# Queries and keys kept in DRAM by feature, with the heads' rows side by side

## The reference

```
xn = adaln(x, cond, ln1);  q, k, v = split(xn @ qkv_w.T);  q, k = rope(q), rope(k)
x  = x + attn(q, k, v) @ sa_out_w.T
xn = adaln(x, cond, ln2);  q = rope(xn @ q_w.T);  k = rope(context @ k_w.T);  v = context @ v_w.T
x  = x + attn(q, k, v) @ ca_out_w.T
xn = adaln(x, cond, ln3);  x = x + (gelu(xn @ ffn_w1.T + b1) @ ffn_w2.T + b2)
attn: softmax(q k' / sqrt(32)) v for each head;  adaln: LayerNorm, then x (1 + gamma) + beta with gamma, beta from cond
```

## Time and profile before

| what | value |
|---|---|
| median of three runs | 1928.59 us |
| profiled execution, its own time | 1925.28 us |
| its span, first to last instruction | 1923.5 us |
| mean granted clock of TensorE | 0.994 |
| PE busy | 1869.4 us (97%) |
| ACT, DVE, POOL busy | 72%, 67%, 41% |
| DMA packets | 306451, 308.37 MB |

### The profile page before, as it was taken

The page is one execution under the profiler, slowest core; times in us unless marked ns, Lnnn a source line. Parts: engine busy times, 40 slices in busy tenths (PEclk is TensorE's granted clock), DMA queues, the critical chain, the costliest instruction groups (busy, mean ns, idle before and its releaser), DMA issues. The chain is left out here.

```text
span 1923.5 us, 39339 instructions
## 1 busy us (share of the span) xinstructions
PE 1869.4 (97%) x13460; PEld 1630.4 (85%) x13460; DVE 1294.9 (67%) x2250; ACT 1383.3 (72%) x3813; POOL 785.8 (41%) x818
## 2 busy tenths in 40 slices
PE   8899999999998999999999998899999999999999
PEld 7788888888877888888888886688898998989898
DVE  7766676767776677676776776446667666666754
ACT  4777777888876888888888888655666666565654
POOL 3534433443442454454454441013536354444531
PEclk9999999999998999999999999999999999999999
DMA  7666676566576778767668677343232322323130
GB/s 232 195 203 185 204 223 194 177 200 198 165 220 189 204 212 233 201 197 227 199 200 225 198 217 190 109 137 110 78 99 67 99 88 89 95 71 110 45 99 33
DMA packets 306451, 308.37 MB, mean 160 GB/s; under 512 B 21072, under 2 KB 260048, under 8 KB 306256
## 3 DMA queue, kind: packets, MB, share of 16 engines
q1 hardware_dynamic: 304528, 304.47, 53.4%
q10 hardware_dynamic: 1728, 1.39, 0.3%
HBM read 212.46 MB, written 92.27 MB: 158 GB/s over the span
## 5 line engine op out<-in xcount | busy, mean ns | idle before, releaser
L744 ACT ACTIVATE ps_s<-ps_s,neg_max 128x256 f32<-128x256 f32 x1024 | 452.8, 443 | 55.4 <-DVE neg_max L861 48.3
L861 DVE TENSOR_REDUCE neg_max<-ps_s 128x2 f32<-128x512 f32 x512 | 349.3, 687 | 212.8 <-PE ps_s L615 212.4
L758 ACT ACTIVATE prob<-ps_s 128x512 f32<-128x512 f32 x512 | 303.4, 593 | 137.2 <-PE ps_s L634 134.3
L634 PE MATMUL ps_s<-qT,kT 98*128 98x256 f32 x1024 | 211.6, 289 | 24.4 <-DMA qT<-max_rows 21.8
L931 POOL TENSOR_TENSOR rope_c<-rope_c,rope_s 128x256 f32<-128x256 f32 x128 | 98.4, 769 | 330.5 <-DVE rope_s L836 330.5
L615 PE MATMUL ps_s<-kT,qT 96*128 96x256 f32 x1024 | 216.5, 293 | 10.7 <-ACT ps_s L744 8.3
L615 PEld LDWEIGHTS ps_s<-kT,qT 96*128 96x128 f32 x1024 | 169.9, 190 | 60.3 <-ACT ps_s L744 28.4
L605 PE MATMUL ps_g<-xx_hi,w_hi 128*128 128x256 f32 x1024 | 208.1, 285 | 1.4 <-issue 1.4
L634 PEld LDWEIGHTS ps_s<-qT,kT 98*128 98x128 f32 x1024 | 169.3, 191 | 46.9 <-issue 21.0
L744 ACT ACTIVATION_READ_ACCUMULATOR ps_s<-ps_s,neg_max 128x1 f32 x1024 | 207.8, 203 | 0.0
L605 PE MATMUL ps_g<-xx_lo,w_hi 128*128 128x256 f32 x1024 | 205.5, 282 | 0.0
(11 more groups left out here) (155 smaller groups left out, 4654.7 us busy)
## 6 DMA issues: line engine op xcount, KB each, us to landing
kT<-k_turned SPq DMA_DIRECT2D x384, 128.0 KB, 3.1
qT<-q_turned SPq DMA_DIRECT2D x128, 256.0 KB, 3.9
f_raw<-in_w1T SPq DMA_DIRECT2D x124, 256.0 KB, 3.1
k_turned<-rot_hi SPq DMA_DIRECT2D x64, 256.0 KB, 3.2
k_turned<-rot_lo SPq DMA_DIRECT2D x64, 256.0 KB, 2.5
q_turned<-rot_hi SPq DMA_DIRECT2D x64, 256.0 KB, 3.6
q_turned<-rot_lo SPq DMA_DIRECT2D x64, 256.0 KB, 4.1
qT<-q_turned SPq DMA_DIRECT2D x128, 128.0 KB, 3.9
```

The source lines that it names most:

```text
L634: ins = eng.matmul(ps_s[:, score_bank(step), t * L:(t + 1) * L], kT[:, quad % NQ, j, t * P:(t + 1) * P], qT[:, quad % NQ, j, :], start=Tru ...
L744: ins = eng.activation(scores[:, t * L:(t + 1) * L], scores[:, t * L:(t + 1) * L], ACT.Exp, bias=neg_max[G % 2][:, t, j:j + 1], accum_out= ...
L758: eng.activation(prob[:, n % NP, :, :].rearrange("p t l -> p (t l)"), ps_s[:, score_bank(step), :], ACT.Exp).then_inc(exp_done, 1)
L861: eng.tensor_reduce(neg_max[G % 2][:, :, j], ps_s[:, score_bank(step), :].rearrange("p (t l) -> p t l", l=L), AX.X, ALU.max, negate=True). ...
```

## The change

The DRAM tensors are laid out as (item parity, part, feature, head, position), so that the rows of one feature of neighbouring heads lie side by side. A spill is then two transfers for the high part and two for the low part, one for each half of the features: source 128 partitions of 1 KB, destination 8 heads x 16 features x 1 KB, with the heads outermost. A stack of queries is one transfer of 64 rows and one of 32 rows, in pieces of 4 KB. A stack of keys is one transfer whose source is the high part, repeated twice by an outermost dimension of size 2 and step 0, into 64 partitions, and one of 32 rows for the low part. The counts of the semaphores follow: 64 for an item's spills and not 32, two transfers for a stack of keys and not three.

```diff
-        turned = {m: nc.dram_tensor(f"{m}_turned", (2, D, 2, L), F32, kind="Internal").ap() for m in "qk"}
+        turned = {m: nc.dram_tensor(f"{m}_turned", (2, 2, HD, H, L), F32, kind="Internal").ap() for m in "qk"}
...
-            STACKS = {"q": 2, "k": 3}
+            STACKS = {"q": 2, "k": 2}
...
-                return spilled[m][t], 32 * (i + 1)
+                return spilled[m][t], 64 * (i + 1)
...
-                        out_to = turned[m][i % 2, T * t * P:T * (t + 1) * P].rearrange("(p d) s l -> s p d l", d=2)
+                        heads = slice(t * HG, (t + 1) * HG)
                         eng.wait_ge(rot_hi_done, n)
-                        eng.dma_start(out_to[0], rot_hi[:, n % NT, :, :].bitcast(F32)).then_inc(spilled[m][t], 16)
+                        for half in range(2):
+                            into = turned[m][i % 2, 0, half * HALF:(half + 1) * HALF, heads, :].rearrange("d h l -> h d l")
+                            eng.dma_start(into, rot_hi[:, n % NT, half, :].bitcast(F32)).then_inc(spilled[m][t], 16)
                         eng.wait_ge(rot_lo_done, n)
-                        eng.dma_start(out_to[1], rot_lo[:, n % NT, :, :].bitcast(F32)).then_inc(spilled[m][t], 16)
+                        for half in range(2):
+                            into = turned[m][i % 2, 1, half * HALF:(half + 1) * HALF, heads, :].rearrange("d h l -> h d l")
+                            eng.dma_start(into, rot_lo[:, n % NT, half, :].bitcast(F32)).then_inc(spilled[m][t], 16)
...
-                        eng.wait_ge(spilled[m][n // 2], 32 * (i + 1))
+                        eng.wait_ge(spilled[m][n // 2], 64 * (i + 1))
...
-                        heads = turned[m][i % 2][n * OH * HD:(n + 1) * OH * HD]
+                        high, low = (turned[m][i % 2, part, :, n * OH:(n + 1) * OH, :].rearrange("d j l -> d (j l)") for part in range(2))
+                        into = (qT if m == "q" else kT)[:, quad % NQ, :, :].rearrange("p h l -> p (h l)").bitcast(F32)
                         if m == "q":
-                            eng.dma_start(qT[0:2 * HD, quad % NQ, :, :].bitcast(F32),
-                                          heads.rearrange("(h d) s l -> (d s) h l", d=HD)).then_inc(stack_in[m][n], 16)
-                            eng.dma_start(qT[2 * HD:ROWS, quad % NQ, :, :].bitcast(F32),
-                                          heads[:, 0].rearrange("(h d) l -> d h l", d=HD)).then_inc(stack_in[m][n], 16)
+                            both = turned[m][i % 2, :, :, n * OH:(n + 1) * OH, :].rearrange("s d j l -> (s d) (j l)")
+                            eng.dma_start(into[0:2 * HD, :], both).then_inc(stack_in[m][n], 16)
+                            eng.dma_start(into[2 * HD:ROWS, :], high).then_inc(stack_in[m][n], 16)
                         else:
-                            for s in range(2):
-                                eng.dma_start(kT[s:2 * HD:2, quad % NQ, :, :].bitcast(F32),
-                                              heads[:, 0].rearrange("(h d) l -> d h l", d=HD)).then_inc(stack_in[m][n], 16)
-                            eng.dma_start(kT[2 * HD:ROWS, quad % NQ, :, :].bitcast(F32),
-                                          heads[:, 1].rearrange("(h d) l -> d h l", d=HD)).then_inc(stack_in[m][n], 16)
+                            eng.dma_start(into[0:2 * HD, :], high.unsqueeze(0).broadcast_to([2, HD, OH * L])).then_inc(stack_in[m][n], 16)
+                            eng.dma_start(into[2 * HD:ROWS, :], low).then_inc(stack_in[m][n], 16)
```

## The result

| kernel | median | ratio to before, 95% interval | span | granted clock |
|---|---|---|---|---|
| before | 1927.6 us | 1 | 1923.5 us | 0.994 |
| the change | 2336.4 us | 1.2116 [1.2091, 1.2140] | 2335.4 us | 0.921 |

The account below looks back on a forecast made before the run. PE bounds the kernel before; after the change, DMA engines 0 and 1 were to bound attention. Start 36, attention 1553 and feed-forward 688.5 give 2277.5 us; with 1.8 and 3.3 us added, 2283 us, range 2150 to 2440.

Parts of the forecast that it names:

- On how many engines a transfer runs: DMA transfers: the smaller outermost count rules; high keys on two engines, spills on eight, queries and low keys on 16.
- Narrow transfers share their engines: Narrow DMA transfers always land on the same first engines, giving engines 0 and 1 34.6 MB in attention.
- Two full engines set the pace: Attention: engines 0 and 1, 96% full at 23.2 GB/s, stretch it to 1553 us; chance 0.60.
- the rival on `max_rows`: `max_rows`, on the same two engines, is held behind high keys once per group: 362 us more, 2583 us; chance 0.10.
- What PE would wait for: Attention: PE's waits for DMA kT at L615 become the largest item, hundreds of us.
- PE's busy time unchanged: Whole kernel: PE stays busy for near 1870 us.
- SyncE's queue at nothing: Attention: 256 more spill issues and 128 fewer for keys, 77 us more issuing, priced at nothing.
- Spills: ScalarE's L719 waits for spills, which stand behind high-key transfers some 6 us more; landings over 5 us.
- spills wide: Rival: spills avoid the narrow limit, engines 0 and 1 have 4096 KB less, total 2095 us; chance 0.12.
- DMA share and rate: Attention: the mean DMA share falls to near 0.5, at some 155 GB/s.
- the feed-forward part: The stretch after attention touches none of the change and stays at 688.5 us.
- separate queues as a reason against: Argument against `max_rows` being held: its other queue may get its turn between pieces; that rival's chance 0.10.

Follow-up runs that it names:

- e1: The changed kernel with the high keys' repeated dimension moved inside, so their transfer runs on 16 engines; 1989.6 us, 1.0314.
- e8: The kernel of e3, with the keys' copies outermost (two engines) for even quads only; 2296.9 us, 1.1917.
- e9: The kernel of e3, with the keys' copies outermost (two engines) for odd quads only; 2182.8 us, 1.1330.
- e4: The changed kernel without the transfer of `max_rows` and its waits, two rows held constant; 2270.1 us, 1.1759.
- e2: The changed kernel with partitions of a half ordered (feature, head), so spills run on 16 engines and keys stay on two; 2303.3 us, 1.1927.
- e10: The kernel of e8 without the transfer of `max_rows` and its waits, two rows held constant; 1998.8 us, 1.0369.
- e4b: The kernel before the change, without the transfer of `max_rows` and its waits, rows constant; 1907.2 us, 0.9892.
- e3: The changed kernel with both differences, key copies inside and spills over 16 engines; 1941.7 us, 1.0056.
- e5: The kernel of e3 with the DRAM tensor split by halves, so each spill is one wide transfer per high or low part; 1933.4 us, 1.0020.
- e6: The kernel of e2 with the keys' repeated transfer, copies outermost, issued on GpSimd's queue with its own semaphore; 2232.1 us, 1.1566.
- e7: The kernel of e6 with the key copies inside, so GpSimd's transfer runs on 16 engines; 1950.0 us, 1.0101.

## Why the prediction was right, and where not

The forecast of 2283 us is 2.3% below 2336, inside its own range of 2150 to 2440. By its steps:

- **On how many engines a transfer runs: right.** Two for the high keys, eight for the spills; the packets of the changed kernel close to the unit with these counts, and e1 takes 347 us back by the order of dimensions alone. The rule of the Trainium skill (DMA: Bandwidth & Descriptors, Why a DMA increments its semaphore by 16 and not by 1) thus agrees with the counts of this trace for 2 of 2 and 16, 2 of 2 and 64, and 8 of 8 and 128.
- **Narrow transfers share their engines: fits, but isn't shown.** The trace names no engine. But a 16 KB transfer on two engines of another queue is held where a narrow key transfer stands just ahead of it (e8) and much less where it doesn't (e9). `max_rows` was never sent on other engines, so whether the shared engines hold it or something that the queues of SyncE and ScalarE share ahead of them stays open.
- **Two full engines set the pace: half right.** By the count of bytes they are near full in the changed kernel (21.5 GB/s of 23.2, 93%, for a forecast of 96%) and in e4 (95%), where `max_rows` is gone. The 23.2 is no firm ceiling: pieces of 4 KB ran at 25.5 in the stretch shown (10% more, where the range allowed 5%), and slower beside other traffic (234 ns on average, for 163 there). So "near full" rests on the count and on the bound of 95%. But the step took this for the only limit. e2 and e8 have 4096 and 11264 KB less on these engines and are faster by 33 and 39 us alone, at 19.3 and 14.7 GB/s. (The 22016 KB in the expectation of e8 leave out the 512 KB of `max_rows`; 22528 is right.)
- **What failed is how the rival on `max_rows` was put together.** I added 362 us to the full engines (2583 us) and gave it 0.10. Its place was right and its size not far off: 209 to 262 us of waits, 278 to 298 us by e8, e10 and e4b. The two limits lie side by side and don't add: without `max_rows` the kernel stays at 2270, with the two engines near full by the count, and with two thirds of the bytes `max_rows` holds it near 2300. So the forecast's number is in part luck: the second limit happens to give nearly the same time as the one that the sum went by, and so it doesn't show in the total. Removing or easing either brings 33 to 66 us, which is why both looked harmless in a first experiment.
- **What PE would wait for: wrong.** I named the keys at L615; the rows show 208.7 us for `max_rows` and 65.4 for the queries. A narrow transfer has no landing in these rows, so a wait for the keys, if there was one, may stand under the queries issued behind them; that is argued and not seen.
- **PE's busy time unchanged: wrong.** It rose from 1159.3 to 1297.2 us in attention, at a granted clock of 0.89 for 0.99. These 138 us are a third of the loss. The forecast put the whole loss down to idle time: 394 us idle, where it was 312. The lower clock comes with the waits: in the group shown it stood at 1.0 before PE's wait of 3.5 us and averaged 0.63 behind it. No run takes the clock apart from the waits.
- **SyncE's queue at nothing: near.** Four spill issues for two are e3 less e5, some 6 us and within noise.
- **Spills:** the wait of ScalarE at L719 came as forecast, 126.1 us. Wide spills alone in place of narrow are worth 33 to 48 us; the case "spills wide" had put them at 188.
- **DMA share and rate** (0.5 and 155 GB/s forecast, 0.51 and 149 measured) and the feed-forward part (690.5 and 690.4 us from the last weights on; the earlier trace rows starts 2 us later) came out.

Still open: what sets e9's 2183 us, with the engines at 16.0 GB/s by my count and `max_rows` nearly in time (33.5 us). The waits name the queries' stack, issued right behind the narrow keys, but no run takes that wait away. Nor was it tried to move `max_rows` itself to a wide form.

## What to carry to other kernels

Read a DMA's outermost dimension on both sides before its piece size: a repetition placed outermost ran on two engines, and putting the same repetition inside won 347 us back. The mean DMA share fell while the kernel got slower; count packets, completion reports included, to see on how many engines each transfer ran. Look also for the small transfer that something waits for: it suffers first, from another queue too, and when it and the bytes are both at the limit, taking away one of the two shows little (here 33 to 66 us of some 400).

## What the hardware showed that I had not expected

- A narrow transfer delays a small narrow one of another queue: by the medians 6.2 us from issue to last report for 1.7, and most of the delay comes before the first piece. I had counted separate queues as a reason against. The Trainium skill (DMA: Bandwidth & Descriptors, Issuing engines are not separate DMA queues) says that DMAs of different issuers interleave on the same engines. The trace agrees in part: in the group shown the pieces of both queues run in turn from 722.01 us on, but none of `max_rows` ran before the narrow key transfer had ended, 3.6 us after its issue.
- Pieces of 4 KB for 1 KB, on as many engines and with as many spills, changed the time by 0.2% (e5), though the queue has 75776 packets fewer.
- GpSimd's narrow transfer made many more packets than its wide one at the same bytes (e6, then e7), 448 for each of 128. By the trace the extra ones are all of 4 bytes (59392 for 2048), while both have 8192 pieces of 4 KB. No run says what they are for.

```profile
q0 software_dynamic: 67584, 33.79, 6.9%
```
```profile
q0 software_dynamic: 10240, 33.56, 6.4%
```
